# Global attention on one core: the value matmuls of a step between the scores of its two query halves

## What is computed

```python
q = rope((x @ Wq).reshape(b, s, 2 * H, hd)).transpose(0, 2, 1, 3) * scaling
k = rope((x @ Wk).reshape(b, s, 2 * H, hd)).transpose(0, 2, 1, 3)
v = (x @ Wv).reshape(b, s, H, 2 * hd).transpose(0, 2, 1, 3)
scores = jnp.einsum('bhqd,bhkd->bhqk', q, k)
probs = jax.nn.softmax(scores, axis=-1).reshape(b, H, 2, s, s)
w = probs[:, :, 0] - lam * probs[:, :, 1]
attn = jnp.einsum('bhqk,bhkd->bhqd', w, v)
```

## Time and profile before

| | |
|---|---|
| median of three runs | 8531.29 us |
| the profiled execution, its own time | 8517.44 us |
| its span, first to last instruction | 8515.8 us |
| TensorE busy (matmuls) | 7618.9 us, 89% |
| VectorE busy | 6957.1 us, 82% |
| ScalarE busy | 6240.2 us, 73% |
| GpSimd busy | 3232.1 us, 38% |
| mean granted TensorE clock | 0.958 of full |

### The profile page before, as it was taken

The page is one execution under the profiler, slowest core; times in us unless marked ns, Lnnn a source line. Parts: engine busy times, 40 slices in busy tenths (PEclk is TensorE's granted clock), DMA queues, the critical chain, the costliest instruction groups (busy, mean ns, idle before and its releaser), DMA issues. The chain is left out here.

```text
span 8515.8 us, 166272 instructions
## 1 busy us (share of the span) xinstructions
PE 7618.9 (89%) x65536; PEld 2763.7 (32%) x65536; DVE 6957.1 (82%) x9027; ACT 6240.2 (73%) x11586; POOL 3232.1 (38%) x4551
## 2 busy tenths in 40 slices
PE   6899978999789988899888998889988899888998
PEld 4322343223432234322343223432234322343223
DVE  5899768997689976899668996689966899768996
ACT  4699746997569965699656996569965699656996
POOL 3344233442334423344233442334423344233442
PEclk9999999999999998999999999999999999989999
DMA  0100001000010000100001000010000100001000
GB/s 30 46 24 21 15 11 46 24 21 19 8 49 21 24 17 5 49 21 24 18 5 49 21 24 20 3 49 21 24 19 3 49 21 24 21 2 49 21 25 21
DMA packets 219177, 205.43 MB, mean 24 GB/s; under 512 B 108087, under 2 KB 143415, under 8 KB 218359
## 3 DMA queue, kind: packets, MB, share of 16 engines
q1 hardware_dynamic: 218364, 194.46, 8.1%
HBM read 123.83 MB, written 67.37 MB: 22 GB/s over the span
## 5 line engine op out<-in xcount | busy, mean ns | idle before, releaser
L1355 DVE TENSOR_REDUCE mfull<-ps 128x1 f32<-128x1024 f32 x4096 | 4707.1, 1216 | 329.0 <-PE ps L1277 328.2
L1430 ACT ACTIVATE work<-ps 128x512 f32<-128x512 f32 x8192 | 4398.7, 597 | 377.1 <-PE ps L1299 257.5
L1317 PE MATMUL ps<-work,vbuf 128*32 128x256 f32 x32768 | 2624.3, 392 | 118.6 <-ACT hh L1450 118.6
L1277 PE MATMUL ps<-kop,qop 48*128 48x512 bf16 x8192 | 2489.3, 385 | 48.5 <-DVE mfull L1355 23.8
L1299 PE MATMUL ps<-qop,kop 51*128 51x512 bf16 x8192 | 2488.0, 384 | 1.1 <-DMA qop<-mT 0.8
L1317 PEld LDWEIGHTS ps<-work,vbuf 128*32 128x32 f32 x32768 | 654.4, 108 | 1769.3 <-issue 938.4
L1299 PEld LDWEIGHTS ps<-qop,kop 51*128 51x128 bf16 x8192 | 479.8, 93 | 1642.3 <-ACT work L1430 1526.2
L1381 POOL CAST mpart<-mfull 128x16 bf16<-128x16 f32 x256 | 50.6, 197 | 2465.3 <-issue 2001.5
L249 POOL TENSOR_TENSOR rstd<-rstd,nhalf 128x8 f32<-128x8 f32 x64 | 109.1, 1705 | 1668.3 <-DVE rstd L243 1668.3
L1399 POOL TENSOR_TENSOR work<-work,none 128x16 f32<-128x16 f32 x224 | 650.5, 2904 | 17.9
L445 POOL TENSOR_TENSOR hh<-work,hmask 128x1024 f32<-128x1024 f32 x256 | 516.3, 2048 | 103.4 <-PE ps L373 103.4
(11 more groups left out here) (168 smaller groups left out, 8885.1 us busy)
## 6 DMA issues: line engine op xcount, KB each, us to landing
qop<-scratch SPq DMA_DIRECT2D x512, 64.0 KB
scratch<-work SPq DMA_DIRECT2D x32, 768.0 KB, 4.1
scratch<-hh SPq DMA_DIRECT2D x32, 768.0 KB, 3.7
kop<-scratch SPq DMA_DIRECT2D x256, 96.0 KB
vbuf<-in_x SPq DMA_DIRECT2D x9, 2048.0 KB, 8.4
qop<-scratch SPq DMA_DIRECT2D x512, 32.0 KB
kop<-scratch SPq DMA_DIRECT2D x256, 64.0 KB
qop<-mT SPq DMA_DIRECT2D x1024, 3.0 KB
```

Of the source, the lines that this page charges most:

```text
L1277: pe.matmul(ps[:, b + n, :], qop[r:r + KQ, s, i, t * P:(t + 1) * P], kop[r:r + KQ, s, i, half(n)], start=True, stop=True).then_inc(s_ms, 1)
L1317: mm = pe.matmul(ps[VW * i:VW * (i + 1), OB, cols], vp[:, b, t, (G * gl + i) // 2, :], prob[:, u % PS, i, cols], start=t == 0 and part == ...
L1355: v.tensor_reduce(mfull[:, m // CUT % 2, r // ROWS * G // 2 + i, to:to + 1], ps[:, b:b + NB, :].rearrange("p b n -> p (b n)"), AX.X, ALU.m ...
L1430: act.activation(prob[:, u % PS, hl, :], ps[:, EB[slot % len(EB)], :], ACT.Exp, scale=scale).then_inc(s_ex, 1)
```

## The change

In TensorE's loop, `values(u, n)` is issued right behind the score pair n, where before both parts were tried behind both pairs and behind `turn_maxima`. Since part 0 is due only at odd steps and part 1 only at even ones, it is part 0 that moves: from behind the second score pair of an odd step to in front of it. Part 1 keeps its place; the even steps have no `turn_maxima`.

```diff
                         for n in range(NB):
                             if 0 <= e < LAST:
                                 exp_scores(NB * e + n)
                             if e + AHEAD < LAST:
                                 max_scores(e + AHEAD, n)
+                            if tile_due(e, n) is not None:
+                                values(tile_due(e, n), n)
                         if at(e, TURN) is not None:
                             turn_maxima(at(e, TURN))
-                        for part in range(2):
-                            if tile_due(e, part) is not None:
-                                values(tile_due(e, part), part)
                         if e in LATE:
```

## The result

The changed kernel takes **9274.17 us** (median of 4 runs, 9271.71 to 9279.78), the kernel before 8528.03 us beside it (8507.37 to 8551.28). The ratio is 1.0876, with a 95% interval of 1.0864 to 1.0889. That is 746 us slower, near the 9318 us predicted. The profiled execution has a span of 9269.9 us, 754 more than before.

A forecast was written before the change was run, and what follows sets the result against it. VectorE was taken to set the pace; eight loops of 2.67 us plus 0.64, 0.65 and 0.14 make 22.79 us per 16 steps against 19.51, +787 us in all, so 9318 us. Range 9130 to 9640.

The forecast's parts named there:

- The loop: Over two steps: first max matmul, values, second max matmul, reduction, next first max matmul; lengthened from 2.02 to 2.67 us.
- The last link: From the end of a reduction to the next max matmul: 0.14 us, behind a reduction of 1.21 us.
- The three interruptions: Output copy, early turn and turn of the maxima, in every 16 steps: +0.64, +0.14 and +0.65 us.
- the copy of the output: At e mod 16 = 3, values wait for ScalarE's copy ahead of the second score pair: +0.64 us.
- the early turn: At e mod 16 = 9, 0.59 us of TensorE, mostly inside its 0.45 us of waiting: +0.14 us.
- the turn: Turn of the maxima, e mod 16 = 11: ScalarE's copy and the next max matmul come later, +0.65 us.
- The sum: Sixteen attention steps take 22.79 us against 19.51, or 0.41 more per odd step: +787 us in all.
- the count of 240 odd steps: Odd steps with values and maxima, 243 in a pair without the first three at half clock; 240 x 8 x 0.41 us.
- What bounds the kernel before: In the attention VectorE sets the pace: sixteen reductions, 18.13 us, plus three stalls, 1.37; only what makes it wait counts.
- Rival 1: The clock falls too in the attention; a quarter of pairs at half clock: +630, some 9,950 us; chance 0.10.
- Rival 2: Values fill the wait ahead of the turn, so VectorE's 0.41 us stalls go: -102 us, 8430; chance 0.05.
- Rival 3: In the attention the later second half is absorbed, and gain and loss in the turn cancel: 8531 us; chance 0.04.

## Why the prediction was right, point by point

- **The loop.** It is there, with the links as read: first max matmul to second 0.89 us (0.88 predicted), second to the reduction 0.45 (0.44). The last link was read too long: 1.28 us from the start of a reduction to the next max matmul, where I had 1.21 + 0.14 = 1.35, from a place where only maxima ran. So the loop is 2.625, not 2.67 us. This is the largest mis-sized term: 8 x 0.045 = 0.36 us in 16 steps.
- **The three interruptions.** 3.20, 2.89 and 3.29 us against plain 2.625 are, in sum, 1.51: +0.58 for the copy of the output, +0.27 for the early turn and +0.67 for the turn. Predicted were 0.64, 0.14 and 0.65, or 1.43. The early turn was priced at half of what it costs, and errors of opposite sign in the terms leave the sum closer than its parts.
- **The sum.** 22.51 us for 16 steps against 22.79. With 1920 odd steps, 3.00 / 8 x 1920 = 720 us against the predicted 787. The spans differ by 754. The trace separates the other 34: eight times the pass without a fall of the clock, 715.6 us from first to last exp matmul against 623.6 before, is 736 us, so 16 us belong to the attention's ends, which the count of 240 odd steps misses. The nine short falls of the clock make 11 us, and 7 lie outside the attention.
- **What bounds the kernel before.** Here the text was wrong. It said that VectorE sets the pace and that only what makes it wait counts, and the halved reduction in the old order disproves that. The forecast survived because it compared the new loop with the measured 19.51 us of 16 steps, whoever sets them. So this part of the agreement is luck: the starting point was measured, and the reason given for it was wrong. Seen from TensorE, its unhindered 2.215 us for two steps became 2.625, and 8 x 0.41 = +3.28, while the interruptions, 1.78 us before, now cost 1.51. That gives +3.01.
- **Rival 1, the clock.** The granted clock stayed at 1.00 over the 550 us shown, with a wait in every second step. The clock did cost something all the same: nine short falls worth 11 us here, and some 50 and 30 us in the variants with both maxima and with both exp scores first, by a longer half clock at the attention's start. By the Trainium skill (TensorE: Matmul & The Clock Gate, "A second HAM failure mode: psum-queue depth-cycling"), in a kernel that cycles through PSUM banks, short idle times of TensorE between groups of matmuls, if frequent enough, make the clock swing between its two levels. This trace agrees only in those few falls.
- **Rival 2, faster by the turn.** The mechanism does not exist in this form: values ahead of the turn alone give 0.9998. Some of that idle time could be won once the turned maxima went into the other bank of the pair, together with the values ahead of the turn.
- **Rival 3, no change.** Excluded. The slack of the two bank pairs did not cover the 0.66 us added.
- **Foreseen only in part, at the turn.** Late exp scores seem to delay ScalarE's copies in general. They cost little in the changed kernel, but most likely the 94 us with the halved reduction in plain steps and a part of the 155 us at the interruptions of the variant with both maxima first.

## What to carry to other kernels

With two buffers, the time from the first write into a buffer to its release must stay below two steps of work, so anything put between the two halves of a producer lengthens a loop that had slack before. Add up that loop link by link before moving work into it. When two engines are both nearly full and each one's sums explain the period, the sums don't say which one binds: shorten one engine's work in an experiment, as the halved reduction did here.

## What the runs showed of the hardware

- Two matmuls on different halves of the array's rows run at the same time even when they were not issued as a pair. In the variant with both exp scores ahead, a max matmul and the exp matmul behind it start within 0.01 us (1657.75 and 1657.76) and take no second slot.
- A wait of some 0.4 us in every 2.6 us of a busy TensorE did not lower the granted clock over the 550 us shown. Over the eight passes it came with nine short falls that the kernel before does not have there, worth 11 of 754 us.
- The half clock can stay for long while TensorE is busy again. In the variant with both maxima first, TensorE was busy 2.62 of 5 us (6006 to 6011 us), and the granted clock was still 0.50 from 6020 to 6080 us, with TensorE busy 59.69 of these 60 us. In six of the eight passes of this run full clock was back some 20 us or less after it fell.
- From the start of a 128 x 1024 reduction out of PSUM to the next matmul that waits for it, 1.28 us pass here. The reduction's own row is 1.22 us long in the mean, so the hand-over costs 0.06 us, less than half of the 0.14 that the rows before suggested.
